# Layer 0 of a four-layer graph network: 15 gathered tiles replaced by row-by-row fetches on SyncE and ScalarE

## The reference

```python
src, dst = (edge_index[0], edge_index[1])
e = edge_attr @ We + be
msg = jax.nn.relu(x[src] + e)
aggr = jax.ops.segment_sum(msg, dst, num_segments=x.shape[0])
h = (1.0 + EPS) * x + aggr
h = jax.nn.gelu(h @ W1 + b1, approximate=False)
return h @ W2 + b2
...
x = _layernorm(x + _L0_gnn_ref(x, edge_index, edge_attr_16, ...), axis=-1)
```

## Time and profile before

| what | value |
|---|---|
| median of 3 runs | 8175.43 us (8169.3 to 8176.95) |
| profiled execution | 8184.69 us, span of its trace 8183.3 us |
| mean granted TensorE clock | 0.835 |
| POOL busy | 5285.2 us, 65% of the span |
| PE busy | 5765.4 us, 70% |
| DVE busy | 4654.3 us, 57% |
| ACT busy | 2316.8 us, 28% |
| Layer 0 in the trace | about 0 to 920 us; its last group reaches line 784 at 917.48 us |

### The profile page before, as it was taken

One profiled execution on the slowest core, in us unless ns is written; L12 is line 12 of the kernel. 1 busy time (PEld: TensorE's weight loads), 2 busy tenths in 40 slices (PEclk: granted clock), 3 DMA queues, 4 the chain that ended last, 5 costly groups with the idle time before them and its releaser, 6 DMA issues.

```text
span 8183.3 us, 141625 instructions
## 1 busy us (share of the span) xinstructions
PE 5765.4 (70%) x50188; PEld 5286.3 (65%) x50188; DVE 4654.3 (57%) x8857; ACT 2316.8 (28%) x6265; POOL 5285.2 (65%) x5490
## 2 busy tenths in 40 slices
PE   5878635887466666478885999988779999823333
PEld 3666535886466665377773889886769999722333
DVE  7777535776487887388884777764122222333333
ACT  0000023443143343044441666651011111112221
POOL 7777777777777776777777777777740000077776
PEclk9989767998588887599995999995889999966666
DMA  5554123332255553133323777762559888711111
GB/s 186 181 171 131 32 69 76 81 79 60 71 145 153 145 147 86 45 86 89 87 76 87 219 218 221 219 168 79 221 228 359 337 335 334 271 29 28 28 28 27
DMA packets 433760, 1151.73 MB, mean 141 GB/s; under 512 B 153430, under 2 KB 227031, under 8 KB 395735
## 3 DMA queue, kind: packets, MB, share of 16 engines
q0 software_dynamic: 225664, 471.04, 23.1%
q1 hardware_dynamic: 205596, 671.39, 22.6%
q10 hardware_dynamic: 1792, 0.23, 0.0%
HBM read 1018.79 MB, written 120.93 MB: 139 GB/s over the span
## 4 chain that ended last, share of the span: by engine, by line
PE 34%; POOL 30%; issue 16%; DVE 11%; DMA 5%; ACT 2%; DVEq 1%; ACTq 0%; SPq 0%; POOLq 0%
POOL pool L1580 16%; PE ps L2282 10%; PE ps L1544 10%; POOL ACC L522 5%; POOL cnt_d L900 5%; PE ps L541 3%; PE ps L1225 2%; DVE ACC L497 2%; POOL pool L522 2%; PE ps L1830 2%; DMA pool<-d_h,srcT_s 2%; ACT ACC L1497 1%; DVE pool L1433 1%; POOL edge_d L1337 1%; DVE pool L1381 1%
## 5 line engine op out<-in xcount | busy, mean ns | idle before, releaser
L1544 PE MATMUL ps<-pool 128*106 128x128 f32 (+2 forms) x19344 | 2402.4, 283 | 50.0 <-DVE pool L1433 50.0
L1544 PEld LDWEIGHTS ps<-pool 128*106 128x106 f32 (+2 forms) x19344 | 2294.6, 170 | 60.3 <-DVE pool L1433 59.8
L1497 ACT ACTIVATE ACC<-ps 72x256 f32 (+1 forms) x2418 | 1012.5, 419 | 1496.2 <-PE ps L1544 1300.8
L522 POOL DMA_INDIRECT ACC<-t,ACC x410 | 387.1, 944 | 1224.4 <-DVE ps L2094 1099.7
L900 POOL DMA_INDIRECT cnt_d<-pool x806 | 843.0, 1046 | 317.2 <-issue 241.2
L1433 DVE TENSOR_TENSOR pool<-pool,ps 128x1024 f32<-128x1024 f32 (+1 forms) x807 | 927.4, 1208 | 0.0
L1580 POOL DMA_INDIRECT pool<-b_h,srcT_s x806 | 765.0, 949 | 245.6 <-issue 232.2
L1580 POOL DMA_INDIRECT pool<-d_h,srcT_s x806 | 764.3, 948 | 245.6 <-issue 177.0
L497 DVE TENSOR_TENSOR ACC<-ACC,ps 65x128 f32 (+1 forms) x1612 | 454.2, 282 | 799.5 <-PE ps L541 573.5
L1580 POOL DMA_INDIRECT pool<-a_h,srcT_s x738 | 708.6, 960 | 224.7 <-issue 215.3
L2282 PE MATMUL ps<-pool,ACC 128*128 128x192 bf16 x8600 | 768.6, 250 | 68.7 <-DMA ACC<-cnt_d 68.7
(11 more groups left out here) (346 smaller groups left out, 8849.6 us busy)
## 6 DMA issues: line engine op xcount, KB each, us to landing
ACC<-cnt_d SPq DMA_DIRECT2D x172, 1600.0 KB, 8.7
pool<-cnt_d SPq DMA_DIRECT2D x88, 1600.0 KB
cnt_d<-pool SPq DMA_DIRECT2D x26, 3200.0 KB, 12.1
ACC<-t SPq DMA_DIRECT2D x1536, 0.2 KB
ACC<-key_d SPq DMA_DIRECT2D x17, 1280.0 KB
ACC<-key_d SPq DMA_DIRECT2D x21, 768.0 KB
ACC<-t ACTq DMA_DIRECT2D x896, 0.2 KB
ACC<-key_d SPq DMA_DIRECT2D x26, 512.0 KB
```

Of the source, the lines that this page charges most:

```text
L522: g.indirect_dma_start(out=gb[b][:, k, :], out_offset=None, in_=table, in_offset=bass.IndirectOffsetOnAxis(ap=idx[:, c:c + 1], axis=0)).th ...
L1497: a.activation(win[:, 0:NPL, bass.ds(reg, 128)], pl[0].rearrange("p (i c) -> p i c", c=128), ACT.Copy).then_inc(*(tile_out if last else A) ...
L1544: mm = t.matmul(o, gbr[:, tile % RT, M * i:M * i + M], oh, start=True, stop=True)
```

## The change

In 15 of the 62 groups the first tile is not gathered by GpSimd. Its 128 rows are fetched one by one with plain DMAs to a strip of on-chip memory (`held_l0`: four strips of 64 columns, two for SyncE, two for ScalarE), and a further DMA moves the strip to slot 0 of the group's buffer. SyncE has nine such groups (17, 22, 27, 33, 38, 43, 49, 54, 59), ScalarE six (20, 28, 36, 44, 52, 60). From iteration 7 on, SyncE issues 24 rows an iteration (up to iteration 54) in three runs of eight, each behind a load of eight row numbers; ScalarE issues 16 in an iteration (7 to 54), behind one load of sixteen. A tile is moved four (SyncE) or five (ScalarE) iterations ahead of its group. TensorE waits for the move beside the gathers.

```diff
+ROWS_FROM, SP_ROWS, ACT_ROWS = 7, 24, 16
+SP_L0 = [u for u in (ROWS_FROM - (-128 * (i + 1) // SP_ROWS) + 4 for i in range(NG)) if u < NG]
+ACT_L0 = [u for u in (ROWS_FROM + 128 * (i + 1) // ACT_ROWS + 5 for i in range(NG)) if u < NG]
+L0_STAGED = SP_L0 + ACT_L0
...
-                for k in range(tiles(gi)):
+                for k in range(first(gi), tiles(gi)):
...
+        def first_gathered(gi):
+            return 1 if gi in L0_STAGED else 0
...
+        held_l0 = [wl[:, 1388:1452], wl[:, 1452:1516], wl[:, 1516:1580], wl[:, 0:64]]
...
+        def sync_rows_l0(gi):
+
+            for e0 in range(SP_ROWS * (gi - ROWS_FROM), SP_ROWS * (gi - ROWS_FROM + 1), 8):
+                i, p0 = e0 // 128, e0 % 128
+                if e0 >= 0 and i < len(SP_L0):
+                    if p0 == 0 and i >= 2:
+                        s.wait_ge(sp_put.sem, 16 * (i - 1))
+                    if p0 == 0:
+                        s.wait_ge(sp_nos_in[i % 2].sem, 16 * (i // 2 + 1))
+                    _, regs = nc.values_load_multi_w_load_instructions(
+                        sp_nos[i % 2][0:1, p0:p0 + 8], engines=[mybir.EngineType.SP], min_val=0, max_val=NP - 1,
+                        skip_runtime_bounds_check_because="sources are node numbers")
+                    for e in range(8):
+                        s.dma_start(held_l0[i % 2][p0 + e:p0 + e + 1, :],
+                                    I["x"][bass.ds(regs[e], 1), :]).then_inc(*sp_staged[i % 2].one())
+                    if p0 == 120:
+                        sync_numbers_l0(i + 2)
+
+        def sync_tile_l0(u):
+
+            i = SP_L0.index(u)
+            s.wait_ge(sp_staged[i % 2].sem, 16 * 128 * (i // 2 + 1))
+            s.wait_ge(eam.sem, 2 * (u - GB0) + 1)
+            s.dma_start(gb0[u % GB0][:, 0, :], held_l0[i % 2]).then_inc(*sp_put.one())
...
         def scalar_l0():
             a.wait_ge(*mark["l0_ready"])
+            scalar_numbers_l0(0)
+            scalar_numbers_l0(1)
...
                 relu.then_inc(*o_l0["msg"].one())
+                if gi + 5 in ACT_L0:
+                    scalar_tile_l0(gi + 5)
+                scalar_rows_l0(gi)
...
                 t.wait_ge(arrived_l0[q].sem, arrivals_l0(gi))
+                if gi in SP_L0:
+                    t.wait_ge(sp_put.sem, 16 * (SP_L0.index(gi) + 1))
+                if gi in ACT_L0:
+                    t.wait_ge(act_put.sem, 16 * (ACT_L0.index(gi) + 1))
...
                 sync_count_rows_l0(gi)
                 if gi % 4 == 0:
                     sync_segments(gi // 4)
+                if gi + 4 in SP_L0:
+                    sync_tile_l0(gi + 4)
+                sync_rows_l0(gi)
...
             gpsimd_gather(I["x"], srcT, gb0, arrived_l0, eam, PARTS, EARLY_GB, mark["l0_ready"],
-                          gathered_tiles)
+                          gathered_tiles, first_gathered)
```

More of the change, by code:

```diff
@@ L507, in gpsimd_tile_flags, with gpsimd_gather @@
                     in_=tile_flag[:, j, :], in_offset=None).then_inc(*flagged.one())
-        def gpsimd_gather(table, idx, gb, arrived, read, parts, free=0, ready=None, tiles=lambda gi: K):
+        def gpsimd_gather(table, idx, gb, arrived, read, parts, free=0, ready=None, tiles=lambda gi: K, first=lambda gi: 0):
             nb = len(gb)
@@ L516, in gpsimd_gather @@
                     gpsimd_tile_flags()
-                for k in range(tiles(gi)):
+                for k in range(first(gi), tiles(gi)):
                     c = gi * K + k
-                    part = [i for i, (k0, m) in enumerate(parts) if k0 == k]
+                    part = [i for i, (k0, m) in enumerate(parts) if max(k0, first(gi)) == k]
                     if part and gi >= nb:
@@ L660, in gathered_tiles @@
             return K - PG if gi >= FIRST else K
+        def first_gathered(gi):
+            return 1 if gi in L0_STAGED else 0
         def arrivals_l0(gi):
-            return 16 * sum(gathered_tiles(x) for x in range(gi % GB0, gi + 1, GB0))
+            return 16 * sum(gathered_tiles(x) - first_gathered(x) for x in range(gi % GB0, gi + 1, GB0))
+        held_l0 = [wl[:, 1388:1452], wl[:, 1452:1516], wl[:, 1516:1580], wl[:, 0:64]]
+        sp_nos, act_nos = ([ns[0:1, 256 * q + 128 * j:256 * q + 128 * j + 128].bitcast(I32) for j in range(2)] for q in range(2))
@@ new lines, in build, with sync_numbers_l0, scalar_numbers_l0 @@
+        sp_nos_in, act_nos_in = ([dsig(f"l0_{q}_numbers{j}_in") for j in range(2)] for q in ("sp", "act"))
+        sp_staged, act_staged = ([dsig(f"l0_{q}_staged{j}") for j in range(2)] for q in ("sp", "act"))
+        sp_put, act_put = dsig("l0_sp_tile_put"), dsig("l0_act_tile_put")
+        def sync_numbers_l0(i):
+            if i < len(SP_L0):
+                s.dma_start(sp_nos[i % 2], I["srcR0"][i:i + 1, :]).then_inc(*sp_nos_in[i % 2].one())
+        def scalar_numbers_l0(i):
+            if i < len(ACT_L0):
+                a.dma_start(act_nos[i % 2], I["srcR0"][len(SP_L0) + i:len(SP_L0) + i + 1, :]).then_inc(*act_nos_in[i % 2].one())
@@ new lines, in sync_tile_l0, with scalar_rows_l0 @@
+        def sync_tile_l0(u):
[3 more added lines that the diff above has]
+            s.dma_start(gb0[u % GB0][:, 0, :], held_l0[i % 2]).then_inc(*sp_put.one())
+        def scalar_rows_l0(gi):
+            e0 = ACT_ROWS * (gi - ROWS_FROM)
+            i, p0 = e0 // 128, e0 % 128
+            if e0 >= 0 and i < len(ACT_L0):
+                if p0 == 0 and i >= 2:
+                    a.wait_ge(act_put.sem, 16 * (i - 1))
+                if p0 == 0:
+                    a.wait_ge(act_nos_in[i % 2].sem, 16 * (i // 2 + 1))
+                _, regs = nc.values_load_multi_w_load_instructions(
+                    act_nos[i % 2][0:1, p0:p0 + ACT_ROWS], engines=[mybir.EngineType.Activation], min_val=0, max_val=NP - 1,
+                    skip_runtime_bounds_check_because="sources are node numbers")
+                for e in range(ACT_ROWS):
+                    a.dma_start(held_l0[2 + i % 2][p0 + e:p0 + e + 1, :],
+                                I["x"][bass.ds(regs[e], 1), :]).then_inc(*act_staged[i % 2].one())
+                if p0 + ACT_ROWS == 128:
+                    scalar_numbers_l0(i + 2)
@@ L665, in by_products, with scalar_tile_l0 @@
+        def scalar_tile_l0(u):
+            i = ACT_L0.index(u)
+            a.wait_ge(act_staged[i % 2].sem, 16 * 128 * (i // 2 + 1))
+            a.wait_ge(eam.sem, 2 * (u - GB0) + 1)
+            a.dma_start(gb0[u % GB0][:, 0, :], held_l0[2 + i % 2]).then_inc(*act_put.one())
         def by_products(u):
@@ L802, in sync_l0 @@
             s.wait_ge(*zeroed.now())
+            sync_numbers_l0(0)
+            sync_numbers_l0(1)
             for gi in range(NG):
@@ L2560 @@
         arr[name] = pad(a[x], NT * 128).reshape(NT, 128)[[K * gi + K - 1 for gi in ROW_GROUPS + ACT_GROUPS]].reshape(1, 128 * NROW)
+    arr["srcR0"] = pad(a["src"], NT * 128).reshape(NT, 128)[[K * gi for gi in L0_STAGED]]
     arr["ewT"] = lay_t(a["edge_weight1"][:, 0])
```

## The result

The changed kernel takes 8296.15 us (median of 4 runs, 8287.53 to 8298.24) against 8172.36 us before (8165.77 to 8176.95, 4 runs): a ratio of 1.0151, 95% interval 1.0135 to 1.0167, **124 us slower**. The forecast was 8250 us, in a range of 8166 to 8315.

What follows compares the result with a forecast made beforehand. POOL's gathers, closely followed by TensorE, bound Layer 0; SyncE's 9.8 + 3.3 + 1.9 + 0.5 + 0.5 = 16.0 us an iteration would exceed both, adding 75 us to 8184.7: 8259.8, less 9.3 for the median, about 8250 us (8166 to 8315).

Steps and rivals of the forecast that it cites:

- SyncE's lead: Layer 0: SyncE issues `ea` only one group ahead; at 16.0 us an iteration that margin is gone by about group 14.
- SyncE's period: Layer 0, iterations 7 to 54: SyncE's time per iteration, 16.0 us (14.0 to 17.9), over TensorE's 12.8 and POOL's 14.1.
- Rows and loads together: SyncE, per iteration: 24 rows at 0.408 us, 9.8 us, plus three loads of eight row numbers, 3.3 us.
- The load: SyncE's load of eight row numbers, taken at 1.1 us each; three were bounded by 2.2 to 4.3 us.
- What was there before: SyncE's earlier issues per iteration (`ea`, fill, key row, lines 411 and 417), 1.9 us with gaps.
- The moves: SyncE's tile moves, number lists and the wait for last rows to land: 0.5 us an iteration, between 0.1 and 0.5.
- The held issues: SyncE's rows issuing slower behind each fill, priced from line 417's excess of 2.8 us: 0.5 us an iteration, 0 to 1.4.
- the prediction's own formula: End of Layer 0: group 61 shifts by 48P - 692.9 us, P being SyncE's period; zero at P = 14.43 us.
- The last six groups: TensorE, from group 55 to 61 after SyncE's last rows: 12.8 us a group, 76.8 us in all.
- Whatever moves group 61 moves all that follows by the same amount: End of Layer 0: a delay of its last group passes undiminished to the degree counts and everything after.
- SyncE keeping up: Rival, Layer 0: SyncE's period is 14.0 us, POOL stays the bound and saves up to 19.3 us, 8156 us; chance 0.12.
- The dear rival: Rival, SyncE: fills hold rows until landed, 8 us in 22 iterations, +229 us, 8404 us; chance 0.05.

## Why the prediction was right, and which terms were off

- **The mechanism held.** SyncE's issuing, `ea` behind it, TensorE waiting for `ea`, POOL standing: each stands in the waits after. The first long wait for `ea`, 8.8 us, ends at 255.7 us on TensorE, about where the prediction had SyncE's lead used up (group 14). That it is the rows on SyncE and not those on ScalarE is shown by the two kernels with one engine's rows alone. One sign came out otherwise: TensorE waits for `ea` at 27 places, mostly in every second group, and not in nearly every group from 14 to 55.
- **SyncE's period** was 17.01 us, forecast 16.0 (14.0 to 17.9). Rows and loads together: 13.13 - 0.42 = 12.7 us in an iteration without a fill, forecast 9.8 + 3.3 = 13.1. The load was priced too high (0.784 us and its gaps for 1.1). What was there before came out as priced, 1.9 us. The moves cost less than the 0.5 us: SyncE's waits for rows to land sum to 3.0 us at three places.
- **The held issues are the term that was mis-sized**: 17.01 - 12.7 - 1.9 - 0.1 = 2.3 us an iteration, forecast 0.5 and bounded by 1.4. The bound was worked out from one transfer that is held once, behind a fill. In fact seven rows behind a fill take about 1 us each (five where a tile move stands ahead of them), and where the store of flags has been held already, three or four rows more are held, by up to 2.2 us. With 48 iterations the 1.8 us too few are 86 us.
- **The size was in part luck.** Without the hold the measured terms give 12.7 + 1.9 + 0.1 = 14.7 us, and the prediction's own formula only +13 us for it. So nearly the whole loss hangs on the term that was given 0.5 us; that the forecast came to +75 us all the same is owed to the loads and moves, priced 0.8 us an iteration too high together, which is 38 us. By this estimate the change would have come out not far from even with no rows held, and the forecast had the direction right with the deciding term at a quarter of its size.
- **The rest of the sum.** Iteration 7 began at 149.0 us instead of 143.5 (+5.5). Line 864 of group 55 followed the issue of `ea` by 970.70 - 965.53 = 5.2 us instead of 4.3. The last six groups took (1037.40 - 970.70) / 6 = 11.1 us each instead of 12.8 (-10.1): with all gathers landed they ran faster than in the stretch I took them from. With the period's 48 x 1.01 = +48.5 us these make 992.6 + 5.5 + 0.9 - 10.1 + 48.5 = 1037.4, which is what the trace has.
- **"Whatever moves group 61 moves all that follows by the same amount"** was off by 7 us. The counts moved by 127.2 us and group 61 by 119.9: before, VectorE's cast (915.20 us) came ahead of group 61's gathers, now it comes behind TensorE's work. In the profiled execution 20 us of this come back between the third and the fourth attention pass (the first gather of initial values of the third starts at 3375.1 before and 3498.9 after, that of the fourth at 4426.7 and 4530.2). The medians, 124 us apart, do not have it; the profiled executions are 8184.69 us before, above its median, and 8287.53 us after, below its own. The other traces say that this is mostly scatter: in all twelve this stretch takes from 1031 us (the changed kernel) to 1052 us (the kernel before), 1050 us in the slower kernel with the fills on ScalarE and 1043 us in the faster one with 16 rows, so most of it does not follow the change.
- **The formula with the measured period** holds across five kernels: periods of 16.25, 16.44, 16.92, 17.02 and 17.35 us go with line 864 of group 61 at 999.4, 1003.5, 1031.0, 1036.6 and 1054.0 us, 54.6 us over 1.10 us of period, 49.6 for the 48 expected.
- **The rivals.** SyncE keeping up was the right picture of the kernels with 16 rows, not of this one. The dear rival, rows held until a fill has landed (8404 us), was wrong in size, but nearer to the nature of the hold than my pricing of it: the hold follows the fill's bytes and ends about when they are moved, but slows each issue instead of stopping them.

## What to carry to other kernels

Before work is moved to an engine that looks idle, add up its whole iteration in program order, with everything that it issues for others, and compare it with the period of the slowest engine: here 17.0 us against 14.1 lost 124 us, and the same work at two thirds of the rows on SyncE gained 23. Add it up as a mean over iterations of every kind: those without a fill, at 13.1 us, would have fitted. A steady excess is paid in every iteration once the lead is used up, however small a single wait looks. Price an issue behind a large transfer by a series of such issues, and not by one.

## What the runs showed of the hardware

- A DMA of 256 bytes takes 0.228 us to issue on SyncE, but about 1 us while a fill of 3200 KB is in flight, for seven in a row (five behind a tile move); the 24 rows of an iteration take 16.8 us instead of 11.8.
- It makes no difference which of the two queues issued the fill (17.0 us for the rows with the fill on ScalarE's), and little into how many pieces it is cut (16.2 to 17.9 us for 512 to 2048). Half the bytes hold the rows for 1.5 to 1.7 us instead of 5.0. The Trainium skill ("DMA: Bandwidth & Descriptors", section on issuing engines that are not separate DMA queues) says that issuing from several engines saves only the sequencer's time, and that this is usually small; here that time is the whole matter, and it is not constant. What in the chip slows the issue is open: no kernel here tells a shared generator of descriptors from a shared path to memory.
- ScalarE's register loads are slowed as well: 48 loads of sixteen numbers have these durations in the changed kernel, where Layer 3's had at most 1203 ns. The longest, 3.7 us and more, all began 4 to 7 us behind the issue of a fill.

```profile
L720 ACTq TENSOR_LOAD <-ns x48: 1182/1424/4019, 175.3 to 957.2; - x48
```
